# A decoder's last cross attention: values as weights with a column of ones, and the output projection taken into the loop

## The reference

```python
def _w8a8_linear(x, w, b):
    qx, sx = _dyn_quant(x)        # s = max(|x|) / 127 by token, q = clip(round(x / s), -127, 127)
    qw, sw = _quant_weight(w)
    y = jnp.einsum('bnc,oc->bno', qx, qw) * (sx * sw[:, 0])
    return y + b
q = _w8a8_linear(x, wq, bq).reshape(B, N, H, D).transpose(0, 2, 1, 3)
k = (cond @ wk.T + bk).reshape(B, L, H, D).transpose(0, 2, 1, 3)
v = (cond @ wv.T + bv).reshape(B, L, H, D).transpose(0, 2, 1, 3)
scores = jnp.einsum('bhnd,bhld->bhnl', q, k) * inv_sqrt_d + mask[:, None]
attn = jax.nn.softmax(scores, axis=-1)
o = jnp.einsum('bhnl,bhld->bhnd', attn, v)
o = o.transpose(0, 2, 1, 3).reshape(B, N, C)
return _w8a8_linear(o, wo, bo)
```

## Time and profile before

| | |
|---|---|
| median of 3 runs | 1791.0 us (1789.62 to 1793.01) |
| the profiled execution, by its own time | 1797.26 us |
| its span | 1795.9 us |
| TensorE, VectorE, ScalarE, GpSimd busy | 83%, 64%, 46%, 43% |
| mean granted TensorE clock | 0.85 |
| the stage's loop in the trace | 1439 to 1589 us |
| from the loop's end to the feed-forward's first matmul | 1589 to 1614.88 us |

### The profile page before, as it was taken

The page is one execution under the profiler, slowest core; times in us unless marked ns, Lnnn a source line. Parts: engine busy times, 40 slices in busy tenths (PEclk is TensorE's granted clock), DMA queues, the critical chain, the costliest instruction groups (busy, mean ns, idle before and its releaser), DMA issues. The chain is left out here.

```text
span 1795.9 us, 27080 instructions
## 1 busy us (share of the span) xinstructions
PE 1496.4 (83%) x8792; PEld 1110.0 (62%) x8792; DVE 1144.2 (64%) x2987; ACT 818.3 (46%) x2138; POOL 765.6 (43%) x1199
## 2 busy tenths in 40 slices
PE   3899997899999948999898694166777689959999
PEld 3567673578888822333476584035555479958888
DVE  2577786255555569988555526886888579963222
ACT  1244443134444338887515313456665468832111
POOL 3388882046555646666422204275455322220000
PEclk8799997799999975555599897587989879968999
DMA  5100000200000025555420000200000020000000
GB/s 218 56 7 7 1 2 12 100 14 6 7 1 1 1 53 92 95 89 94 123 99 1 1 1 27 84 16 1 1 1 1 35 108 2 2 1 1 7 6 12
DMA packets 98379, 62.21 MB, mean 35 GB/s; under 512 B 88896, under 2 KB 93376, under 8 KB 96448
## 3 DMA queue, kind: packets, MB, share of 16 engines
q1 hardware_dynamic: 98240, 60.48, 12.6%
HBM read 38.44 MB, written 1.05 MB: 22 GB/s over the span
## 5 line engine op out<-in xcount | busy, mean ns | idle before, releaser
L101 PE MATMUL banks<-normed_t,arena_a 128*128 128x256 f32 x1120 | 258.9, 387 | 3.0 <-PEq L3244 3.0
L101 PEld LDWEIGHTS banks<-normed_t,arena_a 128*128 128x128 f32 x1120 | 217.1, 195 | 34.7 <-issue 4.1
L446 POOL TENSOR_TENSOR lut_weights<-lut_weights,arena_b 128x536 f32<-128x536 f32 x128 | 179.5, 1402 | 123.8 <-DVE arena_b L436 114.0
L605 POOL TENSOR_SCALAR work<-work,small 128x256 f32<-128x256 f32 (+1 forms) x384 | 175.5, 475 | 85.5 <-DVE small L597 85.2
L101 PE MATMUL banks<-arena_a 64*128 64x512 bf16 (+1 forms) x384 | 161.6, 540 | 30.8 <-PEq L3244 18.7
L1615 ACT ACTIVATE arena_a<-banks,work 128x1024 uint8<-128x1024 f32 x128 | 154.1, 1205 | 47.1 <-DVE work L1553 40.5
L1551 DVE TENSOR_REDUCE work<-banks 128x1 f32<-128x1024 f32 x128 | 155.3, 1214 | 24.3 <-PE banks L101 24.3
L1645 POOL TENSOR_SCALAR arena_a<-arena_a 128x1024 bf16<-128x1024 uint8 x128 | 132.2, 1045 | 65.1 <-DMA arena_a<-arena_a 64.6
L107 PE MATMUL banks<-identity,work 128*128 128x128 f32 x968 | 136.9, 283 | 19.4 <-ACT work L550 7.4
L585 ACT ACTIVATE work<-banks,small 128x256 f32<-128x256 f32 (+1 forms) x258 | 115.3, 458 | 62.5 <-DVE small L572 58.7
L107 PEld LDWEIGHTS banks<-identity,work 128*128 128x128 f32 x968 | 116.2, 149 | 34.8 <-POOL work L605 12.7
(11 more groups left out here) (403 smaller groups left out, 3401.9 us busy)
## 6 DMA issues: line engine op xcount, KB each, us to landing
arena_a<-in_L3f_wg SPq DMA_DIRECT2D x1, 4096.0 KB, 12.6
arena_b<-in_lut_idx SPq DMA_DIRECT2D x8, 268.0 KB, 3.2
arena_b<-in_L_wqn SPq DMA_DIRECT2D x1, 2048.0 KB, 12.0
arena_b<-in_L_wo SPq DMA_DIRECT2D x1, 2048.0 KB, 17.8
arena_a<-in_L_wq SPq DMA_DIRECT2D x1, 2048.0 KB, 7.6
arena_a<-in_L_wo SPq DMA_DIRECT2D x1, 2048.0 KB, 13.0
arena_a<-arena_a SPq DMA_TRANSPOSE x128, 2.5
arena_b<-in_L2f_gv SPq DMA_DIRECT2D x1, 2048.0 KB, 8.3
```

The source lines that it names most:

```text
L101: ins = t.matmul(out, lhs_t, rhs, start=start and i == 0, stop=stop and i == n - 1)
L446: g.tensor_tensor(o, o, lut_t[j % 2], ALU.add).then_inc(*summed.up(c * LUT + j))
L605: ins = g.tensor_scalar(e[:, c], e[:, c], A.rl[n % 2][:, 2 * hh + i:2 * hh + i + 1], 0.0, ALU.mult, ALU.add)
```

## The change

- Groups run batch by batch (`m // GROUPS` is the batch), so that a batch's 16 heads are complete after 8 units.
- The values go to one of six buffers `vs_` with 32 columns a head: 16 features, then a column of ones (set once by GpSimd), the rest zeros. `heads_tensor_of_pair` uses them as weights and the turned probabilities, 256 tokens, as the moving side: the result has a head's features on the partitions and the sum of the exponentials on the 17th. The exponentials lose their accumulator; reciprocal and scaling by unit go.
- ScalarE copies four heads at a time (`heads_copied`), and makes all copies of turned queries and keys (before, half of them).
- By batch and by tile TensorE turns the heads back (`output_turned`), VectorE divides by the sums and finds the scale (`output_divided`), GpSimd makes the integers (`output_integers`). Then they are turned, copied, multiplied by the output weights, scaled, added to the residual with its statistics, and for batches 0 to 2 the next norm is made and turned. All of it stands inside the loop over n, with lags 17 to 28 behind the batch's first unit; the loop is now UNITS + 17 long.
- The stage has one barrier at its end instead of three; the first integers and the loop are no longer set apart. The copy of turned probabilities stands at the head of an iteration on VectorE and ScalarE, one iteration later than before.

```diff
-    def mix_tensor(A, n, v_of):
-                ins = products(t, o, [(A.pt[(2 * n + hh) % 4][:, z * P:(z + 1) * P], v_of(b, 2 * p + hh, j))
-                                      for z, (q, j) in enumerate(A.blocks) if q == i])
...
-        v.reciprocal(A.rl[k], A.ls[k]).then_inc(*vs.up(A.s, "sums", n))
...
-        v.tensor_tensor(o4, banks[6].f[:, 0:4 * A.dv].rearrange("p (h t c) -> p h t c", h=2, t=TB),
-                        bcast(A.rl[k].rearrange("p (h t o) -> p h t o", h=2, t=TB), A.dv), ALU.mult).then_inc(*normed_o.up(A.s, n))
...
-            v.tensor_tensor(s3[:, :, 64:192], p3[:, :, 64:192], bias(gg, 64, 192), ALU.add).then_inc(*vs.up(s, "keys", m))
+            v.tensor_tensor(s3[:, :, 64:128], p3[:, :, 64:128], bias(gg, 64, 128), ALU.add).then_inc(*vs.up(s, "keys", m))
+            v.tensor_tensor(vs_[m % 6].rearrange("p (t h c) -> p t h c", t=TB, h=HG)[:, :, :, 0:HD],
+                            by_head(p3[:, :, 128:192]), by_head(bias(gg, 128, 192)), ALU.add).then_inc(*vs.up(s, "values", m))
...
+        def heads_tensor_of_pair(u):
+            m = u // 2
+            t.wait_ge(*(yield p_t_v, s, u))
+            t.wait_ge(*(yield p_t_a, s, u))
+            if u % 2 == 0 and m:
+                t.wait_ge(*(yield o_t_a, s, m - 1))
+            for j in range(TB):
+                for hh in range(2):
+                    h = 2 * (u % 2) + hh
+                    ins = t.matmul(banks[6].f[h * HS:(h + 1) * HS, 0:S], vs_[m % 6][:, (j * HG + h) * HS:(j * HG + h + 1) * HS],
+                                   A.pt[(2 * u + hh) % 4][:, j * S:(j + 1) * S], start=j == 0, stop=j == TB - 1)
+            ins.then_inc(*mixed.up(s, u))
...
+        def output_turned(b, i):
+            bank, empty = A.next_bank(("o", b, i), (normed_o, s, b, i))
...
+        def output_divided(b, i):
+            v.wait_ge(*(yield o_in_psum, s, b, i))
+            v.reciprocal(r.rearrange("p (h o) -> p h o", o=1), o4[:, :, HD:HD + 1]).then_inc(*vs.up())
+            v.tensor_tensor(oc[i].rearrange("p (h c) -> p h c", c=HD), o4[:, :, 0:HD],
+                            bcast(r.rearrange("p (h o) -> p h o", o=1), HD), ALU.mult).then_inc(*normed_o.up(s, b, i))
+            v.tensor_reduce(odq[:, n:n + 1], oc[i], AX.X, ALU.max, apply_absolute_value=True).then_inc(*vs.up())
+            v.tensor_scalar(odq[:, n:n + 1], odq[:, n:n + 1], *CROSS_SCALE).then_inc(*vs.up())
+            v.reciprocal(oiv[:, n:n + 1], odq[:, n:n + 1]).then_inc(*vs.up(so, "scale", b, i))
...
+        def exponentials(u):
+                    ins = a.activation(e[:, c], e[:, c], ACT.Exp, bias=m[:, 2 * hh + i:2 * hh + i + 1])
...
         def tensor():
+            for n in range(LAST):
+                if 0 <= n - 3 < UNITS:
+                    yield from turns_tensor(n - 3)
+                if 0 <= n - 4 < UNITS:
+                    yield from scores_tensor(n - 4)
+                if 0 <= n - 7 < UNITS:
+                    yield from heads_tensor_of_pair(n - 7)
+                if n < UNITS and n % 2 == 0:
+                    yield from project_tensor(n // 2)
                 for i in range(TB):
+                    if (b := output_at(n, 17, i)) is not None:
+                        yield from output_turned(b, i)
+                if (b := output_at(n, 21)) is not None:
+                    yield from integers_turned(b)
+                if (b := output_at(n, 23)) is not None:
+                    yield from out_tensor(b)
...
+                if 0 <= n - 5 < UNITS:
+                    yield from probability_turns_tensor(A, n - 5)
...
         def vector():
+            for n in range(LAST):
+                if 0 <= n - 6 < UNITS:
+                    yield from probability_turns_vector(A, n - 6)
                 for i in range(TB):
+                    if (b := output_at(n, 18, i)) is not None:
+                        yield from output_divided(b, i)
+                if (b := output_at(n, 24)) is not None:
+                    yield from out_vector(b)
+                if 0 <= n - 4 < UNITS:
+                    yield from added_maxima(n - 4)
...
         def gpsimd():
+            for r in vs_:
+                g.memset(r, 0.0).then_inc(*gs.up())
+            for r in vs_:
+                g.memset(r.rearrange("p (h c) -> p h c", c=HS)[:, :, HD:HD + 1], 1.0).then_inc(*gs.up())
```

More of the change, by code:

```diff
@@ L2620, in narrow_scores_tensor @@
             ins.then_inc(*scored.up(A.s, u, hh))
-    def narrow_tensor(N, project, empties, mask_tile=None):
-        for n in range(UNITS + 6):
-            if 0 <= n - 3 < UNITS:
-                yield from narrow_turns_tensor(N, n - 3)
-            if 0 <= n - 4 < UNITS:
-                yield from narrow_scores_tensor(N, n - 4, empties, mask_tile)
-            if n < UNITS and n % 2 == 0:
-                yield from project(n // 2)
-            if 0 <= n - 6 < UNITS:
-                yield from mix_tensor(N.A, n - 6, N.value)
-            if 0 <= n - 5 < UNITS:
-                yield from probability_turns_tensor(N.A, n - 5)
@@ new lines, in scores_tensor @@
+        def scores_tensor(u):
+            qt = A.qt[u % 2]
+            t.wait_ge(*(yield q_t_a, s, u))
+            for hh in range(2):
+                if free := score_bank_free(A, u, hh, masked):
+                    t.wait_ge(*(yield free))
+                for i in range(TB):
+                    ins = t.matmul(score_bank(u, hh)[:, i * S:(i + 1) * S], qt[:, (hh * TB + i) * P:(hh * TB + i + 1) * P],
+                                   qt[:, 512 + hh * S:512 + (hh + 1) * S], start=True, stop=True)
+                ins.then_inc(*scored.up(s, u, hh))
@@ new lines, in integers_copied, with out_tensor @@
+        def integers_copied(b):
+            a.wait_ge(*(yield turned, so, b))
+            if b >= 2:
+                a.wait_ge(*(yield out_made, s, b - 2))
+            a.copy(xot[b % 2], A.bank01["x", b].h[:, 0:KH * S]).then_inc(*xt_a.up(so, b))
+        def out_tensor(b):
+            bank, empty = A.next_bank(("y", b), (vs, so, "y", b))
+            t.wait_ge(*(yield empty))
+            t.wait_ge(*(yield xt_a, so, b))
+            for i in range(TB):
+                ins = products(t, bank.f[:, i * D:(i + 1) * D],
+                               [(xot[b % 2][:, k * S + i * P:k * S + (i + 1) * P], wqt[1][:, k * D:(k + 1) * D]) for k in range(KH)])
+            ins.then_inc(*out_made.up(s, b))
@@ new lines, in out_vector @@
+        def out_vector(b):
+            v.wait_ge(*(yield out_made, s, b))
+            y = A.bank01["y", b].f
+            for i in range(TB):
+                n = b * TB + i
+                v.scalar_tensor_tensor(yb[b % 2][:, i * D:(i + 1) * D], y[:, i * D:(i + 1) * D], odq[:, n:n + 1], swb[1],
+                                       ALU.mult, ALU.mult).then_inc(*vs.up())
+            vs.all(so, "y", b)
+            v.wait_ge(*vs.now())
+            v.wait_ge(*(yield gs, s, "x", b))
+            finish(s, b, yb[b % 2])
@@ L3086, in sync @@
             load(11)
-            yield from meetings(3)
+            yield MEET
         return tensor, vector, scalar, gpsimd, sync
```

282 lines of the change are left out of this document (150 added, 132 removed).

## The result

The changed kernel takes 1809.35 us (median of 4 runs, 1807.26 to 1811.1) against 1792.01 for the kernel before in the same rounds: ratio 1.0096, 95% interval 1.0076 to 1.0116, **17 us slower**. The prediction of 1775 and its range to 1791 are both missed.

What follows compares the result with a forecast made beforehand. In the last cross attention's loop TensorE and VectorE were both taken to be at the limit, before a serial tail. Loop -1.2 and tail -15.0 made -16 us, from a median of 1791.0 to 1775; range 1764 to 1791.

Steps and rivals of the forecast that it cites:

- Where the new waits are: Last cross attention's loop: projections wait for divisions at banks 0 and 1; 0.3 us a pair allowed, giving 8.7.
- first phase: Loop steps without batch work: 12 steps at half of ScalarE's 7.77 us a pair, 3.88 each, 46.6 in all.
- Case 5: Rival: slower, the schedule sets the beat through TensorE's queue around banks 0 and 1; +34 us or +16; chance 0.12.
- decision point: Loop: the mean beat at which the decision between faster and slower falls, 4.7 us.
- signs listed as "Wrong": Loop beat over 4.7; idle ending on TensorE's turnings in division iterations; projection wait over 2 us; tail 20 us or more.
- The loads: Loop, engine work a pair without batch work: TensorE 7.08 us, VectorE 6.95, ScalarE 7.77, the fullest.
- some 124: Loop's 31 steps if engines keep perfectly busy with full speed at the start: some 124 us, a gain of 5.
- forecast loop of 128.0 us: First to last probability copy, 31 steps: 128.0 us instead of 129.2, a gain of 1.2.
- The tail: Last probability copy to the feed-forward's first matmul: 15.6 us instead of 30.6, a gain of 15.0.
- The clock: Loop: emptying TensorE lowers its clock and gives back part of the gain, 4 us; inside the range, no rival.

Runs made afterwards that it cites:

- e2: Changed kernel with ScalarE's copy of the four heads out of bank 6 moved ahead of an even iteration's exponentials; 1787.7 us, 0.9972 of the kernel before.
- e3: Changed kernel with ScalarE's exponentials moved ahead of the cast of the next group's queries in even iterations; 1786.68 us, 0.9972 of the kernel before.
- h1: Changed kernel, queue orders untouched, with heads alternating between banks 6 and 7 and scores left two banks; 1784.68 us, 0.9956 of the kernel before.
- e5: Changed kernel with the edits of both e2 and e3; 1779.53 us, 0.9936 of the kernel before.
- h2: e5 with heads alternating between banks 6 and 7 and scores left two banks; 1779.52 us, 0.9926 of the kernel before.
- g2: e5 with the turning of a batch's integers and all that follows it one iteration later; 1779.65 us, 0.9912 of the kernel before.
- e4: Changed kernel without turning back, division, integers, output product and residual add of batches 0 to 2; 1787.78 us, 0.9976 of the kernel before.

## Why the prediction was wrong

**The step that failed** is the allowance for waits in "Where the new waits are": "I take 0.3 us a pair for this and for the three engines near their limits not meeting well: 8.7." It looked for the wait at banks 0 and 1 alone. For `heads_copied` it charged 0.3 us of ScalarE's time, and for the place where it stands nothing; and the 0.3 us for waits went to the pairs with batch work alone, those of the first phase had none. Measured: 9.07 us a pair in the first phase (7.77 forecast) and 11.1 with batch work (8.7), 25 us in the loop. Bank 6 has one tenant at a time, as before; what changed is who empties it. Before, VectorE did, with the scaling (L526) that stands between its reciprocal at 1503.69 and its copy at 1504.03, and was done 0.7 us ahead of the next mix at 1504.76; now it is an instruction behind 1.7 us of exponentials, which stand behind a cast, which waits for the projection, which stands in TensorE's queue behind the heads themselves.

**Case 5**, slower because the schedule and not an engine sets the beat, was the right kind, but I gave it a chance of 0.12 only; its decision point held: the mean beat is 153.1/31 = 4.94 us, above the 4.7 at which the sign turns. Its place was wrong (e2, e3, h1). Of the signs listed as "Wrong", two appeared, the beat over 4.7 and VectorE's idle time that ends on TensorE's turnings (25.3 us); but VectorE waits so in the phase without divisions too, and the projection's own wait never came to 2 us.

**The loads were nearly right.** ScalarE 7.90 us a pair (7.77) in the changed kernel and 7.56 in e5, where it is full, VectorE 6.98 (6.95), heads 1.06 (1.06), copy of queries 1.01 (0.99), copy of heads 0.35 (0.4). The exponentials follow each other after about 0.40 us (four of 0.50 end 1.70 after the first has begun), where 0.49 to 0.51 lay between them with the accumulator's read (1500.98 and 1501.47 before). VectorE's figure is right by some luck: the 6.95 started from 8.17 us of occupied time, while its busy time before was 31.16/33 of 8.36, that is 7.89, which would have given 6.7. TensorE's 41.20/5.5 = 7.49 is above 7.08 only in part because some of it ran at the lower clock: in e2, at clock 1.00, four pairs of the first phase (1460.91 to 1492.94) have 29.09 us, 7.27 a pair. One sum of the prediction is slightly off too: with 2.25 and 2.6 us less its loop would be 123.2 and not "some 124". With the ring opened the forecast loop of 128.0 us came out at 130.6 and 128.5 (e5, h2), and at 122.6 (g2): the small allowance for engines that do not meet well was true of another order of the same instructions.

**The tail** gave 13.0 of the 15.0 us. The timeline of the changed kernel:

```profile
1611.86 0.69 DVE L403 TENSOR_TENSOR residual<-work,residual 128x512 f32<-128x512 f32 x1
...
1613.67 0.22 DVE L2986 RECIPROCAL small<-banks 128x16 f32<-128x16 f32 x1
...
1617.02 0.48 POOL L3002 TENSOR_SCALAR lut_weights<-lut_weights,tiny 128x256 f32<-128x256 f32 x1
1617.59 1.07 POOL L3004 TENSOR_SCALAR big_b<-lut_weights 128x256 bf16<-128x256 f32 x1
...
1624.65 1.19 PE L101 MATMUL banks<-normed_t,arena_a 128*128 128x256 f32 x2 [3.49 <-PEq L3342]
```

Batch 2's output and statistics stand in VectorE's queue ahead of the first division and hold it until 1613.67, when the turnings of both tiles (1610.93 and 1611.88, 0.7 us each) are over; of batch 2 I had named the norm alone, at nothing. With most of batch 2's work left out (e4) the tail took 14.1 us. And the second half of GpSimd's integers (L3004) takes 1.07 us and not 0.5, so that the last tile's integers take 1.64 us (1617.02 to 1618.66) where I had 1.1, and start 0.3 us late behind the first tile's. Luck on the other side: the heads ran at full clock, 1.06 us and not 1.8.

**The clock.** In the changed kernel it was 0.97 and 0.92 in the two phases, and 1.00 in both in e2, h1 and g2, where the wait for bank 6 or its cause was gone; in e3 and e5 the batch phase still had 0.95 and 0.97. TensorE's work in the batch steps took 64.4 us in the changed kernel and 60.7 in e2, so some 4 us of the loss were the clock; it magnified the loss and, since reordering ScalarE's queue alone brought it back, hardly began it. The rule of the Trainium skill (TensorE: Matmul & The Clock Gate, What's actually happening), that the clock is throttled by default and activity releases it, agrees with this.

## What to carry to other kernels

Where a buffer with one tenant changes the engine that empties it, follow the new emptier's queue: write down what stands in front of it, what that waits for, and go on until you are back at the filler or at an engine with slack. The sum along such a ring bounds the beat from below just as the fullest engine's load does, and only the larger of the two is the forecast; here 8.9 against 7.8 us. The order of the links can be read from the yields before anything runs; the 8.9 itself I summed from the trace afterwards. And an order is good or bad only for one ring: the same three lines moved were worth 22 us in one kernel and cost 17 in the other, so that after such a change the order of every queue has to be made anew.

## What the runs showed of the hardware

GpSimd's two passes over the same 256 columns differ by more than twice: multiply and add in f32 0.48 us (L3002), subtract and minimum with a bf16 result 1.07 us (L3004); whether the operations or the result's type cost it was not tried. The heads' passes with 32 columns of weights, two heads in turn, are faster than full-width ones with as many moving columns, both in f32 at clock 1.00: 8 in 1.06 us, against 48 of L101 in 10.00 us (1700 to 1710 of the changed kernel), 0.13 us each against 0.21. And the clock magnifies a wait: after TensorE had waited 2.92 us its next 8 passes took 1.92 us at the lower level, 1.06 at full clock, so that the engine that was late became later still.
